# First attention layer: partial sums kept in PSUM per block of nodes instead of added into SBUF after every slot

## The chip, the cores and the metric

The kernel runs on one NeuronCore of a Trainium2 chip. TensorE (PE) multiplies matrices into PSUM, eight banks of 512 fp32 per partition; VectorE (DVE) and ScalarE (ACT) work elementwise on SBUF and PSUM; GpSimd (POOL) here issues indirect gathers; SyncE (SP) issues the other DMAs. The engines run their own programs and wait for one another on semaphores. The metric is the device time of one execution in microseconds; less is better.

## The reference, cut to what matters

Two graph layers are computed over 3125 nodes and 100000 edges sorted by destination. The change touches the first attention of the second layer (8 heads of 64):

```python
feat = (x @ W).reshape(n_nodes, H, D)
e = leaky_relu(el[src] + er[dst], 0.2)
m = segment_max(e, dst)
ex = exp(e - m[dst])
denom = segment_sum(ex, dst)
out = segment_sum((ex / denom[dst])[:, :, None] * feat[src], dst)
```

The kernel divides last: for each node it sums `ex * [feat, 1]` over the node's edges, 8 heads of 65 columns (520 in all), and the 65th column of a head is the denominator.

## The kernel before, in words

Nodes lie in `NB` = 25 blocks of 128, edges in chunks of 256. A **slot** is one chunk as far as it lies in one block; there are `NS` = 415 slots, about 17 to a block, in rising order of block. The slot stage handles each as follows.

- POOL (`gather_heads`, line 1824) issues two indirect gathers, each of 128 rows of 2080 bytes of `t2`, into one of `NR` = 10 buffers `hpair` (parts of `a3` and `wts`); it waits until TensorE has done slot s - 10 (`head_mm`).
- SP (line 2030) loads the 128x16 exponentials of the slot into `exb`, four slots in a group, up to eight slots ahead (`head_ex`).
- ACT (lines 1365 and 1367) makes the two one-hot matrices of the slot, 128x128 each, with two instructions for each: Abs(iota - destination) into `oht`, then Relu(1 - that) into `oh`, a ring of four slots.
- DVE (line 1170) multiplies the gathered 128x1040 by the exponentials, which it first copies to PSUM, four slots at a time (line 1167).
- TensorE (line 1715) runs four fp32 matrix products of 260 columns, which the profile lists as eight matmuls; with `start` and `stop` a slot's sum stands alone in one of three PSUM regions `pbig`.
- DVE (line 1158, `add_heads`) adds that 128x520 to the row of its block in `acc1` (part of `a0`) at a register address. In its program the add of slot s - 2 stands behind the multiply of slot s.

While the first 163 slots run, TensorE also does 89 **looks** (lines 1630 and 1632, 16 bf16 matmuls of 200 columns each), which pick the source term of edges for the second half of the exponentials; DVE reduces each (line 856) and spreads sweeps, maxima and leaky ReLU of that half (lines 830 to 951) between the slots. Looks and slots take the three regions of `pbig` in turn (`RING`): each use waits until the use three places before has been read. ACT takes the exponential of the second half (`exps(1)`) some slots after DVE has finished; the order of all this is fixed in the program, by `AFTER` (which look follows which slot) and `MARK` (at which slot a step of DVE ended). The edges of the second half are first needed at slot 195. Before the stage `acc1` is cleared by one memset of DVE (line 997) and two of POOL.

Of the kernel before, what the change touches and what calls it, by code (L numbers as in the profile page):

```python
# [13 lines left out]
P = 128  # L14
# [22 lines left out]
W1 = 520  # L37
OT = {8: 3, 1: 4}
# [132 lines left out]
def program(nc, x, src, dst, ew, w1, b1, g1, be1, w2, b2, g2, be2, wp, bp,  # L171
            gw1, al1, ar1, gw2, al2, ar2, out):
    ctx = ExitStack()
    with ctx:
# [33 lines left out]
        br = sb("br", [4, P], I32)  # L208
# [25 lines left out]
        oht = sb("oht", [P, 2, P])  # L234
# [30 lines left out]
        pbig = [ps[:, 1024 * i:1024 * (i + 1)] for i in range(3)]  # L265
        tp = [bank(4), bank(5)]
# [76 lines left out]

        foundb = [t.rearrange("p b w -> p (b w)")[:, 0:128] for t in (stat[:, :, :], den[:, :, :])]
# [67 lines left out]
        head_oh, head_mm, head_add, head_mul, head_ex = (sem(n) for n in ("head_oh", "head_mm", "head_add", "head_mul", "head_ex"))  # L412
        act_elu, act_heads2 = sem("act_elu"), sem("act_heads2")
        pool_clear, pool_own = sem("pool_clear"), sem("pool_own")
        act_own = sem("act_own")
        V = Steps(sem("vector_step"))
        NCONST = 17
# [14 lines left out]
        def block_of(e, regs, s, table):  # L432

            if s % 4 == 0:
                k = s // P
                e.load(regs, table[k:k + 1, s % P:s % P + 4])
            return e.snap(regs[s % 4], min_val=0, max_val=NB - 1)

        def vector(e):
            regs = [e.alloc_register(f"vb{i}") for i in range(4)]  # L440
# [148 lines left out]
            def job(name):  # L589
# [93 lines left out]
                elif kind == "plan":  # L683
                    e.wait_ge(pe_prep, PREP["counts"])
                    e.tensor_copy(smalli[:, 0:NB], mp[1][:, 0:NB]).then_inc(*V.inc("counted"))
                    plan(8, 4, NC, 336, 67, "plan2")
                elif kind == "turned":
# [30 lines left out]
                elif kind == "ndl":  # L718
                    e.wait_ge(pe_prep, PREP[name])
                    e.tensor_scalar(ndl[:, name[1], :], mp[1][:, :], -1.0, None, ALU.mult).then_inc(*V.inc(name))  # L720
                elif kind == "slots2":
                    e.wait_ge(pe_prep, PREP["slots2"])
                    e.tensor_copy(br[:, :], mp[1][0:4, 0:P]).then_inc(*V.inc())
                    e.tensor_copy(cr[:, :], mp[1][0:4, P:2 * P]).then_inc(*V.inc("slots2"))

# [123 lines left out]
            def found(H, i, to):  # L849
# [4 lines left out]
                pp = pbig[i % 3 if H == 1 else RING["look", i][0]][:, 0:per * stride].rearrange("p (t w) -> p t w", w=stride)  # L854
# [100 lines left out]
            def first_half():  # L955
# [40 lines left out]
                e.wait_ge(*V.last())  # L996
                e.memset(acc1[:, 0:3136], 0.0).then_inc(*V.inc("acc clear"))
# [150 lines left out]
            e.wait_ge(pool_clear, 2)  # L1148

            def add_heads(s):  # L1150
                e.wait_ge(head_mm, s + 1)
                if s:
                    e.wait_ge(head_add, s)
                else:
                    e.wait_ge(*V("acc clear"))
                b = block_of(e, regs, s, br)
                d = acc1[:, bass.ds(b * W1, W1)].rearrange("p (u w) -> p u w", u=2)
# [20 lines left out]
            add_heads(NS - 2)  # L1178
            add_heads(NS - 1)
            e.wait_ge(head_add, NS)  # L1180
# [45 lines left out]
        uses = [("look", i_) for i_ in range(LOOKS_A)] + [("look", i_) for i_ in AFTER[-1]]  # L1226
        for s_ in range(NS):
            uses += [("slot", s_)] + [("look", i_) for i_ in AFTER.get(s_, ())]
        RING = {use: (n_ % 3, uses[n_ - 3] if n_ >= 3 else None) for n_, use in enumerate(uses)}
# [4 lines left out]
        def scalar(e):  # L1234
# [119 lines left out]

            exps(0)
            for s in range(NS):
                so = s % 4
                for k in range(2):
                    if s >= 4:
                        e.wait_ge(head_mm, s - 3)  # L1360
                    elif s == 0 and k == 0:
                        e.wait_ge(*V("slots2"))
# [738 lines left out]
```

## Time and profile before

| | us |
|---|---|
| median of three runs | 3218.97 (3212.55 to 3219.84) |
| the profiled execution | 3221.76 |
| its span, first to last instruction | 3218.8 |
| in the span: slots 1 to 164, with looks | 1494 to 1994 |
| slots 165 to 177 | 1994 to 2048 |
| slots 178 to 414, no looks | 2048 to 2733 |
| DVE busy / TensorE busy over the span | 2334.0 / 2639.7 |

The span is followed by stretches in time, since the stages have different limits: the graph convolutions up to about 1250, the scores of the attention to 1490, the slot stage to 2733, the second attention behind it. A slot counts as done when its last matmul ends.

### The profile page before, as it was taken

The numbers are of one execution on the slowest core, as the hardware profiler recorded it, in microseconds if no ns is written. First come the engines' busy times: TensorE is split into PE (matmuls) and PEld (weight loads), VectorE is DVE, ScalarE is ACT, GpSimd is POOL, SyncE is SP. The second block draws the span as 40 slices with busy tenths as digits, with TensorE's granted clock in tenths as the row PEclk, the third lists the DMA queues.
The fourth block names the chain that finished last, engine by engine and source line by source line (L and its number), as shares of the span: only waits on it lengthen the run. The fifth ranks groups of instructions, "written<-read, shape, count | busy, mean of one in ns | idle before, by whom it ended". The sixth has DMA issues, their size and how long they took to land.

```text
span 3218.8 us, 51543 instructions
## 1 busy us (share of the span) xinstructions
PE 2639.7 (82%) x18059; PEld 1978.5 (61%) x18059; DVE 2334.0 (73%) x3121; ACT 1279.2 (40%) x3089; POOL 999.5 (31%) x1235
## 2 busy tenths in 40 slices
PE   4777777999899998886888987777676777866999
PEld 2666665545455555785777776555555555765888
DVE  7999997797334444987777878866666666785786
ACT  6888885020001112003444444444444444403343
POOL 3000000111102223006666666666666664003000
PEclk8999999999999999997999999998889889967999
DMA  4444446434478783215666776666676666052453
GB/s 136 185 171 179 170 180 236 137 115 132 138 241 260 254 261 108 86 50 176 190 186 192 194 196 176 181 188 183 182 188 181 188 183 170 24 182 61 155 164 108
DMA packets 311101, 538.20 MB, mean 167 GB/s; under 512 B 108482, under 2 KB 213460, under 8 KB 310596
## 3 DMA queue, kind: packets, MB, share of 16 engines
q1 hardware_dynamic: 241700, 309.63, 29.3%
q0 software_dynamic: 69152, 225.28, 24.9%
q8 instruction: 152, 2.49, 0.3%
q14 instruction: 97, 0.79, 0.1%
HBM read 420.89 MB, written 115.11 MB: 167 GB/s over the span
## 4 chain that ended last, share of the span: by engine, by line
PE 56%; DVE 27%; issue 5%; ACT 5%; another core or an unknown queue 4%; DMA 2%; POOL 1%; DVEq 0%; SPq 0%; ACTq 0%; POOLq 0%
PE ps L1715 22%; PE ps L1496 14%; PE ps L1703 9%; DVE a L586 8%; PE ps L1632 5%; DVE a L581 3%; DVE a L582 3%; PE ps L1400 2%; DVE a L1158 2%; DVE a L830 1%; ACT oht L1365 1%; PE ps L1630 1%; ACT oh L1367 1%; PE ps L1522 1%
## 5 line engine op out<-in xcount | busy, mean ns | idle before, releaser
L1715 PE MATMUL ps<-a,oh 128*128 128x260 f32 x2008 | 510.8, 408 | 148.8 <-ACT oh L1367 56.9
L1824 POOL DMA_INDIRECT a<-t,mid x502 | 482.5, 961 | 443.6 <-DVE cin L940 167.8
L1365 ACT ACTIVATE oht<-iota,mid 128x128 f32<-128x128 f32 x830 | 333.3, 402 | 639.3 <-PE ps L1715 425.4
L1496 PE MATMUL ps<-a 128*128 128x512 f32 x1200 | 554.4, 602 | 13.2 <-DVE a L763 13.2
L1715 PEld LDWEIGHTS ps<-a,oh 128*128 128x128 f32 x2008 | 390.3, 202 | 251.0 <-ACT oh L1367 110.2
L1158 DVE TENSOR_TENSOR a<-a,ps 128x520 f32 x415 | 286.6, 691 | 286.8 <-PE ps L1715 196.0
L1715 PE MATMUL ps<-wts,oh 128*128 128x260 f32 x1312 | 345.7, 419 | 97.5 <-DVE wts L1170 40.1
L1463 PE MATMUL ps<-a 128*128 128x200 bf16 x1568 | 319.9, 255 | 108.7 <-issue 53.3
L1824 POOL DMA_INDIRECT wts<-t,mid x328 | 312.5, 953 | 187.5 <-issue 79.4
L1715 PEld LDWEIGHTS ps<-wts,oh 128*128 128x128 f32 x1312 | 265.3, 209 | 165.3 <-ACT oh L1367 59.8
L1496 PEld LDWEIGHTS ps<-a 128*128 128x128 f32 x1200 | 218.6, 192 | 220.8 <-issue 214.6
L1774 POOL TENSOR_SCALAR rstd<-mv 128x1 f32<-128x1 f32 x75 | 30.2, 403 | 915.3 <-DVE mv L473 913.0
L1170 DVE TENSOR_TENSOR a<-a,ps 128x1040 f32<-128x1040 f32 x251 | 308.6, 1230 | 2.2
L1465 PE MATMUL ps<-a 128*128 128x100 bf16 x1568 | 297.9, 208 | 0.0
L1466 PE MATMUL ps<-a 128*128 128x100 bf16 x1568 | 297.7, 208 | 0.0
L1703 PE MATMUL ps<-a,wts 128*128 128x257 f32 (+1 forms) x1250 | 277.0, 384 | 21.2 <-DVE wts L1109 21.2
L1703 PEld LDWEIGHTS ps<-a,wts 128*128 128x128 f32 (+1 forms) x1250 | 235.8, 189 | 60.5 <-DVE wts L1109 23.2
L1367 ACT ACTIVATE oh<-oht 128x128 f32<-128x128 f32 x830 | 257.0, 310 | 26.2
L586 DVE TENSOR_TENSOR a<-a,mid 128x4800 bf16<-128x4800 bf16 x98 | 260.5, 2658 | 3.4
L1463 PEld LDWEIGHTS ps<-a 128*128 128x128 bf16 x1568 | 152.6, 97 | 162.8 <-issue 152.5
L1285 ACT ACTIVATE a<-ps 128x400 f32<-128x400 f32 x392 | 194.4, 496 | 69.6 <-PE ps L1466 67.7
L1287 ACT ACTIVATE ps<-mzero 128x400 f32<-128x400 f32 x392 | 198.8, 507 | 12.5
(327 smaller groups left out, 3920.6 us busy)
## 6 DMA issues: line engine op xcount, KB each, us to landing
a<-at_d SPq DMA_DIRECT2D x60, 1280.0 KB, 6.1
at_d<-a SPq DMA_DIRECT2D x49, 800.0 KB, 3.3
mt_d<-a SPq DMA_DIRECT2D x49, 800.0 KB, 4.9
a<-mt_d SPq DMA_DIRECT2D x30, 1280.0 KB, 6.1
a<-trlo_d SPq DMA_DIRECT2D x49, 512.0 KB
ot_d<-a SPq DMA_DIRECT2D x49, 320.0 KB, 6.0
a<-ot_d SPq DMA_DIRECT2D x49, 256.0 KB, 3.3
a<-t,mid POOLq DMA_INDIRECT x502
```

The costliest lines, as they stand in the source:

```text
L586: e.tensor_tensor(mvr[:, r, :, 0:3], bc(mvr[:, r, :, 3:4], five), bc(w, five), ALU.mult).then_inc(*V.inc(("weighted", b)))
L1158: e.tensor_tensor(d, d, pbig[RING["slot", s][0]].rearrange("p (u w) -> p u w", u=2)[:, :, 0:260], ALU.add).then_inc(head_add, 1)
L1170: e.tensor_tensor(bv, bv, col(exps_ps[:, s % 8, :], 65), ALU.mult).then_inc(head_mul, 1)
L1365: e.activation(oht[:, k, :], iota[:, :], ACT.Abs, bias=ndl[:, k, s:s + 1]).then_inc(*own.inc())
L1367: e.activation(oh[:, so, k, :], oht[:, k, :], ACT.Relu, bias=1.0, scale=-1.0).then_inc(head_oh, 1)
L1463: e.matmul(ps[:, bass.ds(c, W2)].rearrange("p (k d) -> p k d", k=2), lo, mvr[:, b % RB, g, 2:4, :, z], start=False, stop=True, skip_group_ ...
L1465: e.matmul(ps[:, bass.ds(c, WC)], lo, mvr[:, b % RB, g, 0, :, z], start=False, stop=True, skip_group_check=True)
L1466: e.matmul(ps[:, bass.ds(c, WC)], lo, mvr[:, b % RB, g, 1, :, z], start=False, stop=True, skip_group_check=True).then_inc(slot_done, 1)
L1496: m = e.matmul(acc[f].rearrange("p (x d) -> p x d", x=8), X[:, hi, P * f:P * (f + 1)], a, start=(hi == 0), stop=end, skip_group_check=True)
L1703: m = e.matmul(bank(u + j)[0:p, 0:D + 1], coef[t % R2][:, P * j:P * j + p], feat2[:, hi, :], start=(hi == 0), stop=(hi == NB - 1))
L1715: t = e.matmul(pbig[b][:, 512 * u:512 * u + 260], oh[:, so, k, :], hrows[2 * r + k][:, 260 * u:260 * (u + 1)], start=(k == 0), stop=(k == 1))
L1824: e.indirect_dma_start(out=hrows[2 * r + k], out_offset=None, in_=t2, in_offset=bass.IndirectOffsetOnAxis(ap=srci[:, k, s:s + 1], axis=0)) ...
```

## The change

It does five things.

1. All slots of a block add into one PSUM region: the matmuls lose `start`, and their address is a register (`acc_at`, 0 or 1024 columns), so that successive blocks alternate between `pbig[0]` and `pbig[1]`. DVE's add and its three-region ring are gone.
2. ACT no longer makes one-hots. It fills a region (`prepare`, line 1365 of the new file) and copies it out into `acc1` when the run of slots has ended (line 1381): a **run** is what one block has in one of two walks over all 25 blocks. The first walk ends at slot `S0` = 178 whatever block that falls in, so that `exps(1)` has a fixed place behind run 24; the second starts at block 0 again, putting back into PSUM what `acc1` holds. There are 50 runs; those without slots are copied out and prepared like the others.
3. DVE makes the one-hots: two tensor_scalar is_equal of 128x128, in a ring of ten (`RO`).
4. TensorE waits for the run's region (`acc_ready`, against a register) and loads two tables of registers every four slots.
5. Looks use `pbig[2]` alone; the memsets of `acc1` are gone; DVE reads a look three slots behind it rather than two.

The diff, cut to its core:

```diff
+RO = 10
+S0 = 178
+RUNS = 2 * NB
...
+        def run_sum(r):
+            return pbig[(r + 1) % 2].rearrange("p (u w) -> p u w", u=2)[:, :, 0:W1 // 2]
...
 (vector)
-                e.wait_ge(*V.last())
-                e.memset(acc1[:, 0:3136], 0.0).then_inc(*V.inc("acc clear"))
...
-            def add_heads(s):
-                e.wait_ge(head_mm, s + 1)
...
-                e.tensor_tensor(d, d, pbig[RING["slot", s][0]].rearrange("p (u w) -> p u w", u=2)[:, :, 0:260], ALU.add).then_inc(head_add, 1)
             for s in range(NS):
-                r = s % NR
+                r, so = s % NR, s % RO
+                if s >= RO:
+                    e.wait_ge(head_mm, s - RO + 1)
+                for k in range(2):
+                    e.tensor_scalar(ohs[so][:, k, :], iota[:, :], ndl[:, k, s:s + 1], None, ALU.is_equal).then_inc(head_oh, 1)
...
-                if s >= 2:
-                    add_heads(s - 2)
-                    for i in AFTER.get(s - 2, ()):
-                        found_b(i)
+                for i in AFTER.get(s - LOOK_LAG, ()) if s >= LOOK_LAG else ():
+                    found_b(i)
...
-            add_heads(NS - 2)
-            add_heads(NS - 1)
-            e.wait_ge(head_add, NS)
+            e.wait_ge(acc_out, RUNS)
...
+        LOOK_LAG = 3
+            u_ = i_ % 3 if i_ < LOOKS_A + len(AFTER[-1]) else 2
...
 (scalar)
+            def prepare(r):
+                phase, b = divmod(r, NB)
+                i = acc1[:, W1 * b:W1 * (b + 1)].rearrange("p (u w) -> p u w", u=2) if phase else bc(mzero[:, :].rearrange("p (a b) -> p a b", a=1), [P, 2, W1 // 2])
+                e.activation(run_sum(r), i, ACT.Copy).then_inc(acc_ready, 1)
...
-                    e.activation(oht[:, k, :], iota[:, :], ACT.Abs, bias=ndl[:, k, s:s + 1]).then_inc(*own.inc())
-                    e.wait_ge(*own.last())
-                    e.activation(oh[:, so, k, :], oht[:, k, :], ACT.Relu, bias=1.0, scale=-1.0).then_inc(head_oh, 1)
-                if s == MARK["less max", 1] + 4:
+            for r in range(RUNS):
+                if r % 4 == 0:
+                    e.load(run_regs, run_end[0:1, r:r + 4])
+                e.reg_alu(run_at, run_regs[r % 4], 1, ALU.max)
+                e.wait_ge(head_mm, run_at)
+                b = r % NB
+                e.activation(acc1[:, W1 * b:W1 * (b + 1)].rearrange("p (u w) -> p u w", u=2), run_sum(r), ACT.Copy).then_inc(acc_out, 1)
+                if r + 2 < RUNS:
+                    e.wait_ge(acc_out, r + 1)
+                    prepare(r + 2)
+                if r == NB - 1:
                     exps(1)
...
 (tensor)
+                e.reg_alu(lim, lim_regs[s % 4], 1, ALU.max)
+                e.wait_ge(acc_ready, lim)
                 e.wait_ge(head_oh, 2 * s + 2)
                 e.wait_ge(head_mul, s + 1)
-                e.wait_ge(*(V("found", 8, before[1]) if before[0] == "look" else (head_add, before[1] + 1)))
...
-                        t = e.matmul(pbig[b][:, 512 * u:512 * u + 260], oh[:, so, k, :], hrows[2 * r + k][:, 260 * u:260 * (u + 1)],
-                                     start=(k == 0), stop=(k == 1))
+                        t = e.matmul(ps[:, 512 * u:512 * u + 2048][:, bass.ds(c, 260)], ohs[so][:, k, :], hrows[2 * r + k][:, 260 * u:260 * (u + 1)],
+                                     start=False, stop=True, skip_group_check=True)
...
 (gpsimd)
-            e.memset(acc1[:, 3136:6400], 0.0).then_inc(pool_clear, 1)
-            e.wait_ge(*V("leaky", 0))
-            e.memset(acc1[:, 6400:], 0.0).then_inc(pool_clear, 1)
...
 (sync)
-            written = min(MARK["less max", 1] + 12, 192)
+            written = S0 + 8
```

DVE in the last part of the slot stage, before: `br` is the table of block numbers, `gh_in7` says that a gather has landed.

```order
L1170 TENSOR_TENSOR wts<-wts,ps 128x1040 [waits gh_in7]
L437 ISA [waits head_add,head_mm]
L1158 TENSOR_TENSOR a0<-a0,ps 128x520
L1167 COPY ps<-exb 128x64 [waits ex_in6,ex_in5,ex_in7,ex_in4,gh_in8]
L1170 TENSOR_TENSOR wts<-wts,ps 128x1040 [waits head_ex]
L437 ISA [waits head_add,head_mm]
L1158 TENSOR_TENSOR a0<-a0,ps 128x520
L1170 TENSOR_TENSOR wts<-wts,ps 128x1040 [waits gh_in9]
```

The same place after (line 1170 of the new file is the one-hot, line 1179 the multiply):

```order
L1170 TENSOR_SCALAR a4<-iota,mid 128x128 [waits head_mm]
L1170 TENSOR_SCALAR a4<-iota,mid 128x128
L1179 TENSOR_TENSOR wts<-wts,ps 128x1040 [waits gh_in7]
L1170 TENSOR_SCALAR a4<-iota,mid 128x128 [waits head_mm]
L1170 TENSOR_SCALAR a4<-iota,mid 128x128
L1176 COPY ps<-exb 128x64 [waits ex_in2,ex_in1,ex_in3,ex_in0,gh_in8]
L1179 TENSOR_TENSOR wts<-wts,ps 128x1040 [waits head_ex]
```

Behind each multiply stood an add that waits for TensorE's slot s - 2; now two one-hots stand ahead of it, which wait for slot s - 10.

TensorE in the part with looks, before:

```order
L1715 MATMUL ps<-a3,oh 128x260 [waits vector_step,head_mul,head_oh]
L1715 MATMUL ps<-a3,oh 128x260 x3
L1715 MATMUL ps<-a3,oh 128x260 [waits head_add,head_mul,head_oh]
L1715 MATMUL ps<-a3,oh 128x260 x3
L1630 MATMUL ps<-small,dst_n 128x200 [waits vector_step]
L1632 MATMUL ps<-tbl,dst_n 128x200 x3
```

and after (ISA is an address worked out from a register):

```order
L1649 MATMUL ps<-tbl,src_n 128x200 x3
L1737 REGISTER_ALU
L1744 ISA [waits head_mul,head_oh,acc_ready]
L1744 MATMUL ps<-wts,a4 128x260 x2
L1744 ISA
L1744 MATMUL ps<-wts,a4 128x260 x2
L1647 MATMUL ps<-small,src_n 128x200 [waits vector_step]
L1649 MATMUL ps<-tbl,src_n 128x200 x3
...
L1735 TENSOR_LOAD acc_at
L1736 TENSOR_LOAD acc_lim
```

The slot's wait for a read of its region is replaced by one for the run's region; every look now waits for DVE's reading of the look before it (`vector_step`).

ACT where the two walks meet, after (before, this engine had only the pairs of lines 1365 and 1367 there):

```order
L1381 ACTIVATE a0<-ps 128x520 [waits head_mm]
L1365 ACTIVATE ps<-a0 128x2x260 [waits acc_out]
L1377 TENSOR_LOAD run_end
L1378 REGISTER_ALU
L1381 ACTIVATE a0<-ps 128x520 [waits head_mm]
L1365 ACTIVATE ps<-a0 128x2x260 [waits acc_out]
L1360 ACTIVATE a1<-a1 128x1564 [waits vector_step] x2
L1378 REGISTER_ALU
L1381 ACTIVATE a0<-ps 128x520 [waits head_mm]
L1365 ACTIVATE ps<-a0 128x2x260 [waits acc_out]
```

The two exponentials of the second half stand between the copies of run 24 and run 25.

## Rows read from the trace of the kernel before

**Rows 1.** Busy time by stretch: start:end, length, then each engine's busy us.

```profile
core 0: us, PE busy (x) PEld busy (x) DVE busy (x) ACT busy (x) POOL busy (x), PEclk, DMA share, GB/s
1494.00:1994.00 500.00, 444.10 (x2730) 372.82 (x2729) 395.73 (x497) 233.16 (x656) 311.23 (x327) 0.97 0.69 190
1994.00:2048.00 54.00, 33.13 (x114) 24.22 (x113) 53.58 (x70) 20.95 (x55) 29.04 (x28) 0.84 0.54 141
2048.00:2733.00 685.00, 494.13 (x1895) 383.56 (x1893) 437.38 (x532) 333.19 (x937) 430.94 (x456) 0.91 0.68 185
```

**Rows 2.** Waits, stretch 2048 to 2733: who waited for whom, us, times, longest.

```profile
ACT oht L1365 <- PE ps L1715: 195.1, 69, 4.6
```

**Rows 3.** Groups of instructions, stretch 2048 to 2733: count, busy us, mean ns, idle before.

```profile
L1824 POOL DMA_INDIRECT a<-t,mid x274 | 258.9, 945 | 146.6 <-issue 71.9 <-PE ps L1715 43.1 <-remote 31.6
...
L1158 DVE TENSOR_TENSOR a<-a,ps 128x520 f32 x237 | 163.9, 691 | 244.6 <-PE ps L1715 160.3 <-remote 74.4 <-issue 9.6
...
L1170 DVE TENSOR_TENSOR wts<-wts,ps 128x1040 f32<-128x1040 f32 x93 | 114.5, 1231 | 0.8
L1167 DVE COPY ps<-exb 128x64 f32<-128x64 f32 x58 | 12.7, 220 | 0.0
```

**Rows 4.** Timeline, 2261 to 2274: start us, length us, engine, line, [idle before].

```profile
2261.90 7.33 PE L1715 MATMUL ps<-a,oh 128*128 128x260 f32 x32
2265.83 1.23 DVE L1170 TENSOR_TENSOR a<-a,ps 128x1040 f32<-128x1040 f32 x1
2268.57 0.95 POOL L1824 DMA_INDIRECT a<-t,mid  x1 [0.30 <-issue]
2270.69 0.40 ACT L1365 ACTIVATE oht<-iota,mid 128x128 f32<-128x128 f32 x1 [4.52 <-PE ps L1715]
2270.81 0.70 DVE L1158 TENSOR_TENSOR a<-a,ps 128x520 f32 x1 [3.75 <-PE ps L1715]
2270.93 0.96 POOL L1824 DMA_INDIRECT a<-t,mid  x1 [1.41 <-PE ps L1715]
```

**Rows 5.** Groups of instructions, stretch 1494 to 1994.

```profile
L856 DVE TENSOR_REDUCE stat<-ps 128x32 f32<-128x800 f32 x44 | 43.4, 987 | 38.1 <-remote 30.1 <-PE ps L1632 6.0 <-issue 1.7
```

**Rows 6.** Busy time by stretch while TensorE does only looks.

```profile
1360.00:1440.00 80.00, 77.32 (x880) 76.19 (x880) 67.65 (x84) 0.00 (x0) 0.00 (x0) 1.00 0.20 55
```

**Rows 7.** Groups in the stretch 80 to 480, matmuls at register addresses, ScalarE's clears and copies.

```profile
L1463 PE MATMUL ps<-a 128*128 128x200 bf16 x1361 | 276.3, 254 | 96.3 <-issue 47.5 <-ACT ps L1287 20.5 <-DVE a L586 20.0
...
L1287 ACT ACTIVATE ps<-mzero 128x400 f32<-128x400 f32 x342 | 173.4, 507 | 10.9
L1285 ACT ACTIVATE a<-ps 128x400 f32<-128x400 f32 x342 | 169.6, 496 | 58.0 <-PE ps L1466 56.3
```

**Rows 8.** Groups in the stretch 2745 to 2790, the same shapes on DVE and ACT.

```profile
L1196 DVE TENSOR_TENSOR a<-a,den 128x512 f32<-128x512 f32 x18 | 12.3, 684 | 0.0
...
L1293 ACT ACTIVATE yt<-ps 128x512 f32<-128x512 f32 x18 | 10.7, 597 | 0.1
...
L1200 DVE TENSOR_SCALAR a<-a 128x512 f32<-128x512 f32 x17 | 7.3, 427 | 1.8
```

**Rows 9.** Timeline, 1462 to 1490, of DVE, POOL, ACT and SP.

```profile
1464.13 3.48 DVE L951 TENSOR_TENSOR a<-a 128x1564 f32<-128x1564 f32 x2
1464.40 2.34 POOL L1824 DMA_INDIRECT a<-t,mid  x1 [0.31 <-issue]
1467.65 1.51 ACT L1353 ACTIVATE a<-a 128x1564 f32<-128x1564 f32 x1 [0.19 <-DVE a L951]
1476.24 0.95 POOL L1824 DMA_INDIRECT wts<-t,mid  x1 [0.30 <-issue]
1476.76 0.29 DVE L1012 TENSOR_TENSOR a<-a,stat 128x128 f32<-128x128 f32 x1
1482.92 2.79 DVE L856 TENSOR_REDUCE den<-ps 128x32 f32<-128x800 f32 x3 [5.87 <-remote]
1484.17 6.96 SPq L2030 DMA_DIRECT2D exb<-ex_d  x10
```

More of the change, by code:

```diff
@@ L342, in program @@
         hrows = [t[:, W1 * k:W1 * (k + 1)] for t in hpair for k in range(2)]
+        run_no = small[0:4, 128:256]
+        ohs = [oh[:, i, :, :] for i in range(4)] + [a4[:, 544 + 256 * i:800 + 256 * i].rearrange("p (k n) -> p k n", k=2) for i in range(RO - 4)]
         foundb = [t.rearrange("p b w -> p (b w)")[:, 0:128] for t in (stat[:, :, :], den[:, :, :])]
@@ L686, in job @@
                     plan(8, 4, NC, 336, 67, "plan2")
+                    e.tensor_scalar(run_endf[:, 0:NB - 1], small[0:1, 65:64 + NB], float(S0), None, ALU.min).then_inc(*V.inc())
+                    e.tensor_copy(run_endf[:, NB:2 * NB - 1], small[0:1, 65:64 + NB]).then_inc(*V.inc())
+                    e.memset(run_endf[:, NB - 1:NB], float(S0)).then_inc(*V.inc())
+                    e.memset(run_endf[:, 2 * NB - 1:64], float(NS)).then_inc(*V.inc())
+                    e.wait_ge(*V.last())
+                    e.tensor_copy(run_end[:, :], run_endf[:, :]).then_inc(*V.inc("run ends"))
                 elif kind == "turned":
@@ L1225, in program @@
             AFTER.setdefault(-1 if i_ < LOOKS_A + 9 else int((i_ - LOOKS_A - 9) * 1.85), []).append(i_)
[L1226 to L1229, printed above, removed]
+        LOOK_LAG = 3
+        RING = {}
+        for i_ in range(len(LOOKUPS[8])):
+            u_ = i_ % 3 if i_ < LOOKS_A + len(AFTER[-1]) else 2
+            before_ = [k_ for k_ in range(i_) if RING[k_][0] == u_]
+            RING[i_] = (u_, before_[-1] if before_ else None)
         MARK, SLOT = {}, [-1]
@@ L1353, in exps @@
                     e.activation(fvs[:, xx:y], fvs[:, xx:y], ACT.Exp).then_inc(act_exp, 1)
+            def prepare(r):
+                phase, b = divmod(r, NB)
+                i = acc1[:, W1 * b:W1 * (b + 1)].rearrange("p (u w) -> p u w", u=2) if phase else bc(mzero[:, :].rearrange("p (a b) -> p a b", a=1), [P, 2, W1 // 2])
+                e.activation(run_sum(r), i, ACT.Copy).then_inc(acc_ready, 1)
             exps(0)
[L1356 to L1362, printed above, removed]
[L1363 to L1368 removed]
+            e.wait_ge(*V("run ends"))
+            for i in AFTER[-1][-3:]:
+                e.wait_ge(*V("found", 8, i))
+            prepare(0)
+            prepare(1)
+            run_regs = [e.alloc_register(f"run_end{i}") for i in range(4)]
+            run_at = e.alloc_register("run_at")
+            for r in range(RUNS):
[9 more added lines that the diff above has]
+                if r == NB - 1:
                     exps(1)
@@ L1617, in look @@
                 nbf = small[:, 0:2 * W].bitcast(BF16).rearrange("p (t w) -> p t w", t=4)
-                b, before = (i % 3, ("look", i - 3) if i >= 3 else None) if H == 1 else RING["look", i]
+                b, before = (i % 3, i - 3 if i >= 3 else None) if H == 1 else RING[i]
                 pp = pbig[b][:, 0:per * stride].rearrange("p (t w) -> p t w", w=stride)
@@ L1625, in look @@
                 if before is not None:
-                    e.wait_ge(*(V("found", H, before[1]) if before[0] == "look" else (head_add, before[1] + 1)))
+                    e.wait_ge(*V("found", H, before))
                 for k in range(m):
@@ L1723, in tensor @@
                     carry_in(1)
-            e.wait_ge(head_add, NS)
+            e.wait_ge(acc_out, RUNS)
             for name, b in HEADS2:
```

62 lines of the change are left out of this document (35 added, 27 removed).

## The prediction

> **What bounds the kernel now.** Read first the busy time by stretch [rows 1]. Slots 1 to 164, with looks beside them, take 500 us, 3.05 a slot; slots 165 to 177 take 54 us with DVE busy for 53.58 of them; the last 237 slots take 685 us, 2.89 each, and there no engine is busy for more than three quarters (PE 494 us, POOL 431, DVE 437, ACT 333). So the last stretch is bound by a loop of waits. The waits [rows 2] and the idle time ahead of groups [rows 3] show which: ACT's first one-hot step stands 195 us for TensorE, and DVE's add 244.6 us, which is 1.03 us a slot. The timeline [rows 4] shows one turn of it. TensorE runs four slots from 2261.90 to 2269.23, slots 252 to 255, 7.33 / 4 = 1.83 us each. DVE ends its multiply at 2267.06 and then stands in the add of slot 253, whose matmuls by that spacing ended near 2265.7; it starts at 2270.81, and ACT, DVE and POOL all start within 0.24 us of one another. TensorE's signal came about 5 us late, 1.2 us after POOL had ended its last gather (2269.52) and stood still. I take from this that TensorE's signals are held back while POOL issues gathers without a pause, and come when it stops. Everything that waits closely on them (DVE's add two slots behind, ACT's ring of four) stops with them.
>
> A milder reading is that only the end of the matmuls is shown too early. The Trainium skill bears on it, Perfetto Trace Analysis, "Tensor Engine Instruction (MATMUL, LD_WEIGHTS)": TensorE's end in a profile is worked out from the instruction's size, not observed. By that rule a slot could really cost TensorE the 2.89 us and the last stretch would not get shorter at all; the row on the looks' stretch speaks against it, where the same matmuls and 0.77 us of looks fit into 3.05 us.
>
> Behind the loop stands POOL: a gather takes 945 ns [rows 3] and 0.30 of issue [rows 4], so 2 x 1.25 = 2.50 us a slot. That is the floor of the last stretch if nothing waits. In the first stretch TensorE comes near too: 1.83 for the slot, and 16 matmuls of a look at 77.32 / 880 = 0.088 us [rows 6], 1.41 us, for 89 looks in 163 slots 0.77 us: 2.60 together.
>
> **What changes, part by part.** I go against the profiled execution, 3221.76 us; the median is 2.8 less, which I take off at the end.
>
> *DVE.* Its add goes, 0.69 us [rows 3], and with it the wait on slot s - 2. Two one-hots come. No row has them: 128x512 of the same operation takes 0.427 us against 0.684 for a two-input one [rows 8], so 0.11 each by its columns alone is the lower end and 0.29, what a two-input 128x128 takes [rows 9], the upper one. I take 0.24 as nearer to the latter, where the fixed part shows, 0.48 for two. DVE has then 1.23 + 0.48 + 0.22 / 4 = 1.77 us a slot, under POOL's 2.50: hidden, except in slots 165 to 177, where it is full, (0.69 - 0.48) x 13 = 3 us gained. It now waits for slot s - 10, as POOL does.
>
> *ACT.* Its four one-hot steps go. No slot waits on it any more but at the walks' seam.
>
> *The last stretch, cadence.* What still waits for late signals is POOL (ten slots deep), DVE's one-hots (ten, two slots behind POOL), and ACT at the end of a run, with a run of 17 slots as cover. POOL issues up to ten slots; a gather lands, is multiplied and used some 3 slots behind. If signals come only when POOL stops, each stop frees about 7 to 8 slots instead of the 4 to 5 now, for a stop of 1.4 us [rows 4] to 2.2. That makes 2.50 + 0.2 = 2.70 us a slot. The lower end is 2.50, the upper 2.89 as now.
>
> *The seam, added.* When slot 177 is done, its block is number 10. ACT must copy out and prepare runs 10 to 33 before region 35, where slot 178 adds: 24 pairs. A pair is two copies of 520 columns: 0.60 for 512 columns [rows 8], 0.61 each, plus 0.09 between (400 columns take 0.50 and 0.51 [rows 7]), 1.31 us; and two exponentials of 1.51 [rows 9]. That is 24 x 1.31 + 3.0 = 34.5 us in which TensorE stands. POOL stands too, its ring being full, until slot 178 is seen, some 4 us more with TensorE restarting on its lower clock. Nothing covers this. Ten slots lie ready then; POOL has 227 to issue, and the last takes 7 us to land, be multiplied, added and copied out. The last stretch is 34.5 + 4 + 7 = 46 (rounded) plus 227 x 2.70 = 613, so 659 us against 685: 26 gained. The cadence at which it would gain nothing is (685 - 46) / 227 = 2.81.
>
> *The first stretch.* The floor is TensorE's 2.60 plus addresses from registers. In the stretch of register-addressed matmuls the idle time ahead of 1361 of them is 47.5 us of issue, at most 96.3 in all [rows 7]: 0.035 to 0.07 each, up to 0.1 a slot for two. Against it, looks have one region instead of a share of three: look i + 1 waits for DVE's reduce of look i, 0.99 us, and that for a signal of TensorE; DVE already stands 38.1 us ahead of 44 of these, 30.1 of them for signals with no clear sender [rows 5], late ones. Two slots, 3.7 us, usually lie between looks, so a signal over 2.5 us late stops TensorE. I take 2.80, between 2.65 and the present 3.05, nearer the lower since the add and ACT's ring no longer stop it: 164 x 0.25 = 41 us gained.
>
> *At nothing.* The memsets that go: DVE waits 5.87 us behind its own [rows 9] and the exponentials' loads only start at 1484.17, so the stage starts when it did. Five small instructions more for the tables stand in DVE's program beside convolution work bound by TensorE. TensorE's two table loads every four slots stand ahead of a wait while 1.83 us of matmuls run; uncovered they would cost what the range of the first stretch has in it. The late load of the small piece is needed only in the second attention.
>
> Sum: 41 + 3 + 26 = 70 us; 3221.76 - 70 = 3152, for the median **3149 us**.
>
> **The rivals.**
> *Freed entirely.* POOL never waits, the first stretch falls to 2.65: 66 + 3 + (685 - 46 - 568 = 71) = 140 us, 3079. For it: ten slots are 25 us and the longest wait of ACT is 4.6 [rows 2]. Against: nothing shows that a hold ends before POOL stops.
> *The gathers set the pace (slower).* Both stretches run near 3 us a slot though TensorE's load differs by 0.77 us; DMA share is 0.69 and 0.68 in both [rows 1]. If the pace belongs to gathers and signals as a whole and stays, the first stretch gains nothing and the last is 46 + 227 x 2.89 = 702, 17 slower, less the 3 of the middle: 3233. The seam decides: above 2.81 the last stretch loses. Against: at 2.50 us a slot POOL has nothing to do for a seventh of the last stretch, so something else holds the pace.
> *The one-hots hold POOL up.* A gather took 2.34 us beside a long two-input operation of SBUF, 0.95 beside one of 0.29 us [rows 9]. Were POOL stopped for all of 0.48 us a slot, it would need 2.98: 11 gained in the first stretch, 3 in the middle, 46 + 676 - 685 = 37 lost in the last: 3242. By the Trainium skill, SBUF — State Buffer, "Who interferes with whom", this is the rule: a VectorE operation in a two-port mode and a GpSimd one lock a shared pair of ports for the whole instruction. The short row disagrees with it, the long one agrees.
> *Looks stop more often.* The single region makes late signals stop every look; the first stretch goes to 3.2, 25 lost, against 29 gained elsewhere: 3215.
> *It does not do what it says.* If slot 178 waited for runs that are ready, the seam would vanish; the order shows the pairs as they were counted, so I give this nothing.
>
> **How the numbers follow.** Forecast 0.50 (its own range 3105 to 3190), freed entirely 0.17, gathers set the pace 0.16, one-hots hold POOL 0.07, looks stop 0.10. The range, 3075 to 3242, leaves out the outer halves of the outer cases and what their unknown costs add. About 0.3%, 10 us, can be told from no change. Faster 0.66, the forecast and the freed case; same 0.11, mostly the looks case; slower 0.23, the two others.
>
> **What would show it.** In the changed kernel's profile: slots 178 to 414 from seam to end at 2.5 to 2.8 us each; a gap of TensorE of 35 to 40 us at slot 178 with ACT full in it; DVE's idle time ahead of multiplies (gathers), no more on TensorE, in the last stretch; one-hots of 0.2 to 0.29 us and gathers still 945 ns; the first stretch at 2.65 to 2.9 with DVE's reduce as its largest wait. The forecast is wrong if POOL still idles 0.4 us a slot, if gathers last over 1.1 us, or if the seam is over 60 us.

## The result, and the profile after

The changed kernel takes 3236.43 us (median, 3228.79 to 3243.24) against 3216.99 us (3210.42 to 3223.03) of the kernel before: a ratio of 1.0062, interval 1.0047 to 1.0078, so slower by about 20 us. The forecast was 3149 us, a gain. The time lies inside the stated range, near its upper end, and the sign is wrong.

Busy time by stretch of the changed kernel's profiled execution (its own time 3237.48 us): start:end, length, then each engine's busy us and instructions, granted TensorE clock, DMA share, GB/s. The stretches are slots 1 to 164, 165 to 177, the seam at slot 178, and the rest.

```profile
core 0: us, PE busy (x) PEld busy (x) DVE busy (x) ACT busy (x) POOL busy (x), PEclk, DMA share, GB/s
1494.00:2004.00 510.00, 445.18 (x2722) 382.80 (x2721) 363.15 (x662) 10.90 (x18) 312.09 (x327) 0.94 0.68 186
2004.00:2052.00 48.00, 31.23 (x109) 22.55 (x107) 44.95 (x73) 1.21 (x2) 34.30 (x28) 0.85 0.60 163
2052.00:2087.00 35.00, 3.93 (x9) 2.86 (x9) 16.84 (x33) 31.17 (x52) 2.03 (x2) 0.50 0.20 65
2087.00:2756.00 669.00, 523.04 (x1889) 409.99 (x1887) 386.75 (x738) 16.36 (x27) 431.50 (x454) 0.85 0.69 185
```

Beside [rows 1]: the first stretch became 10 us longer, not 41 shorter; the second is 5 to 6 shorter; slots 178 to 414 took 685 us and take 35 + 669 = 704. From slot 178 on, the seam included, DVE has 34 us less to do and ACT 286 less, and neither is worth anything. The data rate is 185 GB/s, as before.

Groups of instructions from slot 178 to 414: count, busy us and mean ns, then idle time before them and what ended it.

```profile
L1854 POOL DMA_INDIRECT a<-t,mid x274 | 260.4, 950 | 137.4 <-issue 73.0 <-remote 60.7 <-PE ps L1744 3.7
L1744 PE MATMUL ps<-a,oh 128*128 128x260 f32 x768 | 222.0, 441 | 61.6 <-issue 56.5 <-DVE a L1170 3.8
L1179 DVE TENSOR_TENSOR a<-a,ps 128x1040 f32<-128x1040 f32 x137 | 169.6, 1238 | 125.9 <-DMA a<-t,mid 114.4 <-issue 10.3
L1170 DVE TENSOR_SCALAR a<-iota,mid 128x128 f32<-128x128 f32 x270 | 66.6, 295 | 4.1 <-PE ps L1744 4.1
L1381 ACT ACTIVATE a<-ps 128x520 f32<-128x520 f32 x14 | 8.5, 604 | 648.7 <-remote 442.1 <-PE ps L1744 206.7
```

The waits of [rows 2, 3] have moved as meant: DVE no longer stands for TensorE but for gathers, ACT for ends of runs. But GpSimd's gathers, 950 ns and 0.30 of issue as before, still have stops ahead of them ("remote": a signal for which the profile finds no sender close before it). And TensorE, which hardly waits for anybody now, has 56.5 us of idle time with no cause shown in one group alone.

The timeline round one stop of GpSimd shows both. Start us, length us, engine, line, operation, [idle before, and what ended it]:

```profile
2371.79 5.20 PE L1744 MATMUL ps<-a,oh 128*128 128x260 f32 x23
...
2377.20 0.95 POOL L1854 DMA_INDIRECT wts<-t,mid  x1 [0.30 <-issue]
...
2377.51 0.38 PE L1744 MATMUL ps<-a,oh 128*128 128x260 f32 x1 [0.51 <-issue]
...
2378.45 0.95 POOL L1854 DMA_INDIRECT wts<-t,mid  x1 [0.30 <-issue]
2378.94 0.38 PE L1744 MATMUL ps<-a,oh 128*128 128x260 f32 x1 [1.05 <-issue]
...
2380.35 0.47 PE L1744 MATMUL ps<-a,oh 128*128 128x260 f32 x1 [1.04 <-issue]
...
2381.78 1.36 PE L1744 MATMUL ps<-a,oh 128*128 128x260 f32 x3 [0.96 <-issue]
2382.06 0.95 POOL L1854 DMA_INDIRECT wts<-t,mid  x1 [2.66 <-remote]
2382.93 3.45 PE L1744 MATMUL ps<-a 128*128 128x260 f32 x9
```

The gather at 2382.06 is the first of slot 289 and needs slot 279 done, whose last matmul by this record ended at 2371.30: GpSimd stood from 2379.40, and started 10.8 us after the work that it waited for. Meanwhile TensorE stops between the matmul passes of slot 283, where it waits for no semaphore, four times for 0.5 to 1.05 us. In this trace's records of that semaphore three updates stand together, at 2381.80, 2381.89 and 2381.99, just ahead of the gather: the signals themselves came late and in a bunch. (Some 20 of its 415 records are missing, so they can't be paired one by one.)

Counted over both profiles of each kernel, slots 200 to 414: before, GpSimd stopped 66 and 67 times, started 5.4 and 5.1 us (mean) after the matmuls it needed had ended, and was idle in these stops for 116 and 113 us; after, 47 and 46 times, 10.5 and 10.6 us late, 101 and 102 us. Of each stop 0.30 us is the ordinary time of issue; without it the stops come to 96 and 93 us before and 87 and 88 after. The longer rings of DVE and ACT made fewer and longer stops, and the slot stays at 2.88 us (before 2.90).

The seam, same view: ACT's first pairs and the end of it.

```profile
2052.41 0.60 ACT L1381 ACTIVATE a<-ps 128x520 f32<-128x520 f32 x1 [33.84 <-PE ps L1744]
...
2053.04 0.61 ACT L1365 ACTIVATE ps<-mzero 128x520 f32<-128x520 f32 x1
2053.59 0.59 ACT L1381 ACTIVATE a<-ps 128x520 f32<-128x520 f32 x1
...
2054.74 0.59 ACT L1381 ACTIVATE a<-ps 128x520 f32<-128x520 f32 x1
...
2069.82 2.89 ACT L1360 ACTIVATE a<-a 128x1564 f32<-128x1564 f32 x2
...
2083.44 6.28 PE L1744 MATMUL ps<-wts,a 128*128 128x260 f32 x16 [31.07 <-ACT ps L1365]
...
2087.54 0.95 POOL L1854 DMA_INDIRECT wts<-t,mid  x1 [32.56 <-PE ps L1744]
```

24 pairs of 1.15 and the two exponentials: TensorE begins again at 2083.44, 31.1 us after slot 177 ended (2052.4), and GpSimd at 2087.54, 35.1 us after it.

In the first stretch the waits that grew are those round the looks (who waited for whom: us, times, longest):

```profile
DVE den L874 <- remote: 68.3, 24, 5.5
POOL a L1854 <- PE ps L1744: 63.9, 34, 11.6
...
PE ps L1647 <- DVE den L874: 35.6, 12, 5.5
...
DVE stat L874 <- remote: 32.0, 10, 5.8
...
PE ps L1647 <- DVE stat L874: 18.7, 5, 5.3
```

The same waits in the kernel before, 1494 to 1994:

```profile
DVE stat L856 <- remote: 30.1, 12, 3.8
DVE den L856 <- remote: 18.4, 8, 3.8
PE ps L1630 <- DVE stat L856: 10.0, 8, 2.2
PE ps L1630 <- DVE den L856: 4.9, 5, 2.2
```

DVE's reduces of looks stand 68.3 + 32.0 us for late signals, where they stood 30.1 + 18.4, and TensorE's looks 54 us for these reduces instead of 15. Behind slot 12 alone, a reduce waits 4.74 us and the next look 5.46 for it, and slot 13 ends 11 us after slot 12, where the slots before it took 1.7 to 4.2:

```profile
1530.07 0.99 DVE L874 TENSOR_REDUCE den<-ps 128x32 f32<-128x800 f32 x1 [4.74 <-remote]
1530.40 0.95 POOL L1854 DMA_INDIRECT a<-t,mid  x1 [1.83 <-remote]
...
1531.12 0.35 PE L1647 MATMUL ps<-small,src_n 100*128 100x200 bf16 x1 [5.46 <-DVE den L874]
```

### The profile page after: what moved, and what is told of

Its sections match the earlier page's. It is cut to its first block, busy times and chain, and to the rows that moved or that the text cites. A ratio compares the mean times of both kernels' runs of the same rounds, so it can differ in the third digit from the quotient of the medians.

```text
span 3235.5 us, 50165 instructions
## 1 busy us (share of the span) xinstructions
PE 2677.7 (83%) x18059; PEld 2018.5 (62%) x18059; DVE 2259.8 (70%) x3543; ACT 748.7 (23%) x1529; POOL 1001.8 (31%) x1234
## 4 chain that ended last, share of the span: by engine, by line
PE 46%; DVE 30%; POOL 8%; issue 6%; another core or an unknown queue 5%; ACT 3%; DMA 2%; DVEq 0%; SPq 0%; ACTq 0%; POOLq 0%
PE ps L1513 14%; PE ps L1744 11%; PE ps L1720 8%; DVE a L592 8%; PE ps L1649 5%; POOL a L1854 4%; DVE a L587 3%; POOL wts L1854 3%; DVE a L588 3%; PE ps L1417 2%; DVE a L1179 2%; DVE a L848 2%; DVE wts L1179 2%; PE ps L1647 1%
## 5 line engine op out<-in xcount | busy, mean ns | idle before, releaser
L1744 PE MATMUL ps<-wts,a 128*128 128x260 f32 x1312 | 356.6, 423 | 100.5 <-issue 58.9
L1744 PE MATMUL ps<-a,oh 128*128 128x260 f32 x1344 | 365.5, 424 | 65.0 <-issue 56.5
L1744 PEld LDWEIGHTS ps<-wts,a 128*128 128x128 f32 x1312 | 274.4, 213 | 165.9 <-issue 120.4
L1744 PEld LDWEIGHTS ps<-a,oh 128*128 128x128 f32 x1344 | 280.8, 212 | 131.0 <-issue 84.3
L1381 ACT ACTIVATE a<-ps 128x520 f32<-128x520 f32 x50 | 29.8, 596 | 1207.0 <-PE ps L1744 662.6
L1179 DVE TENSOR_TENSOR wts<-wts,ps 128x1040 f32<-128x1040 f32 x164 | 202.5, 1235 | 86.6 <-DMA wts<-t,mid 73.6
L1744 PE MATMUL ps<-a 128*128 128x260 f32 x664 | 175.8, 414 | 34.2 <-issue 27.0
```

The costliest lines, as they stand in the source:

```text
L1179: e.tensor_tensor(bv, bv, col(exps_ps[:, s % 8, :], 65), ALU.mult).then_inc(head_mul, 1)
L1744: t = e.matmul(ps[:, 512 * u:512 * u + 2048][:, bass.ds(c, 260)], ohs[so][:, k, :], hrows[2 * r + k][:, 260 * u:260 * (u + 1)], start=Fals ...
```

## The experiments

Two theories. **Held signals** (the forecast's): TensorE's signals are held while GpSimd issues without a pause, so whoever stands further back from them loses less. **The gathers' pace** (the rival): something about the gathers allows one slot in 2.88 us, and late signals are how it reaches GpSimd; what one wait loses, another gets. It turned out that the runs met two levels of time for the same program, which became the sharpest comparison of all: the kernel before took 3217, 3215.8 and 3218.9 us on some chips (**late chips**: the first traces', and those that the record numbers 7 and 5), and 3006.6, 3008.2 and 3009.8 on others (**prompt chips**: 9, met twice, and 12). Whether that belongs to the chip itself or to something else that differed there, no run shows. Every ratio below is to the kernel before on the same chip. The changed kernel as it stands was never timed on a prompt chip; the nearest is no_ex below, 3023.93 against 3006.59, so an estimate is 0.6% slower there too.

**The kernels themselves, again.** First the changed one, then the one before, both on a late chip; then the one before on a prompt chip.

> The changed kernel unaltered, timed and profiled again. On the chip of the four runs before, TensorE's signals were not held back: all slots beside gathers took 2.50 to 2.52 us, at GpSimd's floor, and the kernel before took 3006.6 us. If this chip is of that kind: 3024 to 3028 us against 3006 (a ratio of 1.006), slots of 2.51 in both stretches and 34.8 us at slot 178. If it is of the kind of the first traces: 3236 against 3217, slots of 2.88.

> The kernel before unaltered, for its profile on the same chip. Where signals are not held: 3006 us, and the question is where 2.50 is reached. If held signals were the only thing that kept the kernel before from GpSimd's floor, its last 237 slots take 2.50 us each (593 us) with nothing for the change to gain there, and its first 164 about 2.60, so that the change gains 15 us in the first stretch, 3 in the middle and loses 35 at the seam. Where they are held: 3217, slots of 2.89 and 3.05.

Measured: 3234.06 us against 3215.76, ratio 1.0046 (1.0029 to 1.0064); the profiled execution of the kernel before took 3213.39. The last stretch repeats (706 against 684 us from slot 178 to 414). The first lost more, 513 against 495 us where it had been 511 against 500 (from the end of slot 0 to that of slot 164), and the middle gained more, 45 against 57 us.

> The kernel before, for its profile on a chip without holding, 3007 us. If held signals were all that kept it from GpSimd's floor, its last 237 slots take 2.50 us each and the first 164 about 2.55; then the change had nothing to gain there but what ScalarE's and VectorE's rings cost, under 0.1 us a slot, against 35 at the seam. If VectorE's add two slots behind stops it even without holding, its slots are above 2.6. On a chip with holding: 3215 and 2.87 to 2.9.

Measured: 3009.01 us. Stretches of this execution, slots 1 to 164, 165 to 177, 178 to 414:

```profile
1492.00:1909.00 417.00, 414.66 (x2729) 365.97 (x2727) 398.74 (x499) 233.05 (x656) 310.55 (x326) 1.00 0.81 228
1909.00:1963.00 54.00, 33.69 (x111) 24.37 (x110) 53.55 (x68) 21.53 (x55) 32.61 (x29) 0.84 0.55 146
1963.00:2542.00 579.00, 465.23 (x1895) 340.60 (x1895) 445.62 (x531) 332.72 (x936) 432.39 (x456) 1.00 0.79 219
```

The same program, with the same durations (a gather 948 ns, TensorE's slot 1.75 us at full clock), gives 2.51 us a slot from slot 200 on: GpSimd's 2 x 1.25, with no stop at all, and the recorded signals of TensorE's slots stand 14 ns behind the end of the last matmul. Slots 1 to 164 take 2.54 with 89 looks among them. So where signals are prompt the kernel before is already at the floor in both stretches, DVE's add and ACT's ring of four cost it nothing, and the change has little but the middle to gain. TensorE's granted clock in the last stretch is 1.00 here; on late chips, where TensorE has its idle times, it is 0.91 and 0.90 before and 0.85 after.

**The seam.** One walk over the blocks; the second exponentials stand at the place where this graph lets them (run 9 ends with slot 168, run 10 with slot 185), so this version is fitted to this data.

```diff
-RUNS = 2 * NB
+RUNS = NB
...
-                if r == NB - 1:
+                if r == 9:
                     exps(1)
```

(The two tables are made without `S0`.)

> The changed kernel with one walk over the 25 blocks: 25 runs, no run ends at slot 178, and ScalarE's second exponentials stand behind run 9, whose block ends with slot 168 in this graph (so it is fitted to this data). Both theories on the pace agree here, it tests the seam: 24 empty pairs x 1.31 us and two exponentials, 34.9 us in the changed kernel's profile, go, and the pace of the slots stays. Expected 3236 - 32 = 3204 us (3198 to 3210), so 13 us under the kernel before; no gap of TensorE over 5 us at slot 178. If what follows the seam had gained from it (ten slots lie ready, 227 instead of 237 are left to fetch), up to 28 us of the gap come back and the time is about 3225 to 3230.

Measured: 2994.34 against 3006.59, ratio 0.9958 (0.9945 to 0.9972), on a prompt chip. Three more runs of it, the last on a late one:

> The changed kernel with one walk (25 runs, second exponentials behind run 9), as in the first call, for a chip on which signals are held. The seam of 34.8 us goes and the pace stays 2.88 us for the 236 slots from 178 on (a pace set by held signals asks for no seam): 3234 - 32 = 3202, 14 under the kernel before. But ten slots lay ready behind the seam and went at 1.78 us each; without the seam these 11 us come back: 3213, about the kernel before. On a chip without holding: 2994 against 3006.

> The changed kernel with one walk (25 runs, second exponentials behind run 9), once more for a chip on which signals are held. If the seam simply adds to the pace: 3234 - 32 = 3202, a ratio of 0.996. If what lay ready behind the seam (ten slots at 1.78 us) was a gain that came from it: 3213, 0.999 to 1.001. On a chip without holding: 0.995 as in the two calls before.

Measured, prompt again: 2993.75 (0.9946, 0.9930 to 0.9963) and 2995.93 (0.9957, 0.9943 to 0.9971).

> The changed kernel with one walk, once more for a chip on which signals are held. If the seam simply adds to the pace: 3234 - 32 = 3202, a ratio of 0.996. If what lay ready behind the seam (ten slots at 1.78 us) was a gain that came from it: 3213, 0.999 to 1.001. On a chip without holding: 0.995, as three times before.

Measured on a late chip: 3203.53 against 3218.91, ratio 0.9949 (0.9931 to 0.9967). Its last stretch (POOL busy, clock, share and GB/s are the last five numbers):

```profile
2046.00:2723.00 677.00, 525.33 (x1898) 412.85 (x1896) 403.45 (x771) 19.39 (x30) 436.63 (x458) 0.84 0.69 187
```

677 us against 704 and 706, and 3203.53 us in all against 3236.43 and 3234.06 of the changed kernel on other late chips: the whole is 31 to 33 us shorter, as the seam alone would have it (3202 to 3204), and not 3213. In the last stretch itself 27 to 29 us of the seam's 31 to 35 show. GpSimd stops 44 times, 10.5 us late, 2.89 us a slot. Without the seam the rest of the change is worth 15 us on a late chip and 12 to 14 on a prompt one. This beats both kernels.

**Whose pace it is.** All of these take something out from slot 200 on, and fit the waits to it. First on a prompt chip: no gathers, and, in a run of its own, no loads of exponentials.

```diff
-            for s in range(NR, NS):
+            for s in range(NR, 200):
                 gather_heads(s)
```

> The changed kernel without the gathers of slots 200 to 414, which use the rows that lie in their buffers: everything else of a slot is done. Slots 200 to 414 took 2.88 us each. If signals are held back by gathers, or gathers set the pace, the slots fall to TensorE's or VectorE's own time, 1.83 to 2.0 us: 215 x 0.95 = about 200 us less, 3035. If TensorE's matmuls really last longer than the profile shows and gathers don't matter, they stay at 2.6 to 2.9 us: 3180 to 3240.

Measured: 2858.70 us, one execution; from slot 200 to 414 it took 375 us, 1.75 each. That is TensorE's own time for a slot, with DVE beside it. The expectation had been written for a late chip.

> The changed kernel without SyncE's loads of exponentials from slot 200 on (old ones are used). If these loads of 64-byte pieces and SyncE's register work are what slows signals or gathers, the slots fall to 2.50 to 2.60 us: 60 to 80 us less, 3155 to 3175. If it is gathers alone, 2.85 to 2.9 us stay: 3225 to 3240.

Measured: 3023.93 us; 2.51 a slot. The loads set nothing there; on a late chip this wasn't tried.

Then half of the matmuls, on a prompt and on a late chip:

```diff
-                for u in range(2):
+                for u in range(2 if s < 200 else 1):
                     for k in range(2):
                         t = e.matmul(...)
```

> The changed kernel without the second half (columns 260 to 519) of the matmuls of slots 200 to 414. If signals are held until GpSimd stops, the number of matmuls has no part in it: 2.8 to 2.9 us a slot, 3220 to 3237. If TensorE's own true pace beside gathers is 2.88 us and the end in the profile is shown too early, the slots fall to GpSimd's 2.50 us: 215 x 0.38 = 81 us less, 3155.

> The changed kernel without the second half of the matmuls of slots 200 to 414, again, for a chip of the other kind. Where signals are not held: 2.50 us a slot as before (3026 us). Where they are: 2.8 to 2.9 (3220 to 3237) by the theory of held signals; 2.50 (3155) if TensorE's true pace beside gathers is 2.88.

Measured: 3025.98 (prompt) and 3226.81 (late, 7 us under the whole one), one execution each. Between the multiplies of slots 210 and 414 a slot took 2.51 and 2.86 us. On the late chip:

```profile
2145.00:2740.00 595.00, 391.58 (x832) 222.89 (x832) 353.64 (x674) 15.13 (x25) 389.44 (x411) 0.62 0.69 189
```

TensorE's granted clock is 0.62 (0.85 with whole slots), so its busy time fell less than its columns; still it is idle for a third of the stretch, and the pace did not move: TensorE's number of matmuls has no part in it, and the "milder reading" of the forecast, that a slot really costs TensorE 2.89 us of matmuls, falls. The next run says the same, with all eight matmuls.

Half of the gathers, on the late chip:

```diff
-                for k in range(2):
+                for k in range(2 if s < 200 else 1):
                     e.indirect_dma_start(...)
```

> The changed kernel with one gather of 128 rows instead of two in slots 200 to 414. GpSimd's floor falls to 1.25 us. Where signals are not held TensorE sets the pace at 1.75 (slots 200 to 414 took 375 us without any gather): 161 us less than the changed kernel. Where signals are held until GpSimd stops, each slot brings half of the holding: 1.8 to 2.0 us a slot, 190 to 230 us less. If bytes moved per time are the limit (532 KB in 2.88 us), 1.75 as well; if TensorE's own true pace is 2.88, nothing is gained.

Measured: 2982.10 us, one execution, 252 less than the changed kernel. That is the case of a limit on the gathers (1.75 us a slot); held signals had 190 to 230 less. Slots 200 to 414:

```profile
2125.00:2500.00 375.00, 375.00 (x1713) 325.07 (x1711) 342.80 (x683) 15.15 (x25) 197.62 (x208) 1.00 0.60 155
```

TensorE is full, 1.75 us a slot, to the microsecond the same as without gathers. The timeline, GpSimd's rows:

```profile
2202.57 0.95 POOL L1855 DMA_INDIRECT a<-t,mid  x1 [0.80 <-PE ps L1745]
...
2204.32 0.95 POOL L1855 DMA_INDIRECT a<-t,mid  x1 [0.81 <-PE ps L1745]
...
2206.07 0.95 POOL L1855 DMA_INDIRECT wts<-t,mid  x1 [0.81 <-PE ps L1745]
```

GpSimd now waits ahead of every gather, for TensorE, and starts 0.27 us after the end of the slot it needs; from slot 225 on it was over 0.5 us late only 8 times in 190. On the same chip, in the same execution, the first stretch was as slow as ever (507 us), but here the lateness is nearly gone, and so are TensorE's stops inside a slot. A gather every 1.75 us is fine; one every 1.25 is what a late chip does not keep up, and it settles at one every 1.44.

**A break or the bytes.** Register operations were meant as a break in GpSimd's issuing:

> One walk, and four register operations of GpSimd behind each slot's two gathers, a break of some 0.1 to 0.3 us in its issuing. If signals pass whenever GpSimd does not issue for a moment, GpSimd never stands for them and the slots take 2.50 plus the break, 2.6 to 2.8: 20 to 90 us less than one_walk2. If only a stop on a wait, or a pause of more than about 0.5 us, lets them pass, the break adds to 2.88 or lies in the stops: 0 to 60 us more. On a chip without holding it costs its length, 415 x 0.1 to 0.3.

> One walk, and sixteen register operations behind each slot's gathers, a break of 0.4 to 1.2 us. By held signals: no stops of GpSimd are left, TensorE's signals come within 1 us of its last matmul's end, and the slots take 2.50 plus the break. If signals stay late by 5 to 10 us even so, it is not GpSimd's issuing that holds them but the traffic of the transfers.

Measured on a prompt chip: 2993.30 (0.9953, 0.9936 to 0.9970) and 2995.31, the time between gathers 0.305 us as without them. They made no break, so these two runs say nothing of the theories. A small operation of GpSimd's own made one:

```diff
+                if s >= 8:
+                    e.wait_ge(pool_pause, s - 7)
+                e.tensor_scalar(pause[:, s % 8:s % 8 + 1], mhalf[:, :], 1.0, None, ALU.mult).then_inc(pool_pause, 1)
```

> One walk, and one small GpSimd operation (128x1, 0.26 to 0.4 us) behind each slot's two gathers, in its own queue of instructions, so that its issuing breaks for that long. Where signals are held: if any break of issuing lets them pass, GpSimd no longer stands for them and a slot takes 2.50 + 0.3 to 0.5 = 2.8 to 3.0, with TensorE's signals no more than one slot late and no stop of GpSimd; if the break is too short or bytes are the cause, stops stay (46 of them, 2 us each) and the slots rise to 3.1 to 3.4. Where they are not held: 2.8 to 3.0, about 150 us more.

Measured on a prompt chip: 3067.13, ratio 1.0202 (1.0185 to 1.0219): 2.69 us a slot in the last stretch, less than the 2.8 to 3.0 expected.

> One walk, and one small GpSimd operation (128x1) behind each slot's two gathers, which made a slot 2.69 us on a chip without holding, 0.19 over the floor. Where signals are held: if a break of issuing of this length lets them pass, GpSimd no longer stands and the slots take 2.69 to 2.75, 0.13 to 0.19 less than now, 30 to 60 us less than one_walk4; if the break is too short or the bytes under way are the cause, its stops stay and the slots take 2.9 to 3.1, 0 to 70 us more. Where they are not held: 3067, as before.

Measured on the late chip of one_walk4: 3211.70, ratio 0.9977 (0.9962 to 0.9991), 8 us over one_walk4; their profiled executions are 3.7 us apart, 2.8 of them in slots 165 to 177. Slots 178 to 414:

```profile
2047.00:2725.00 678.00, 539.86 (x1896) 405.49 (x1896) 402.32 (x771) 18.54 (x29) 502.44 (x686) 0.83 0.70 186
```

This decides between the theories, for the last stretch. On a prompt chip the break adds 0.19 us to each slot; here it adds nothing to the last stretch (678 against 677), and the stops shrink in its place: 31 instead of 44. Without the ordinary idle time ahead of a gather (0.30 us, in this kernel 0.16) they come to 50 us instead of 88, a difference of 38 where 215 x 0.19 = 41 were put in. Signals are not prompter (13.1 us late when GpSimd stops). By held signals either the break should have been added to each slot, 3.08 us, or the stops should have gone, 2.69 to 2.75; it was 2.88. So the time a slot takes is given, and a stop is only what is left of it.

Half of the bytes with the same number of rows (from slot 200 on):

```diff
-                    e.indirect_dma_start(out=hrows[2 * r + k], out_offset=None, in_=t2, ...
+                    e.indirect_dma_start(out=hrows[2 * r + k][:, 0:260], out_offset=None, in_=t2.rearrange("n (h w) -> (n h) w", h=2), ...
```

> One walk, and gathers of rows of 1040 bytes instead of 2080 in slots 200 to 414: the same number of rows and of instructions, half the bytes. If signals are held by GpSimd's issuing: the same pace as one_walk2, 2.85 to 2.9 us. If the bytes under way hold them, or the transfers set the pace: 2.50, 80 us less. On a chip without holding 2.50 in both.

> One walk, and gathers of rows of 1040 bytes instead of 2080 in slots 200 to 414, same number of rows and instructions. Where signals are held: 2.85 to 2.9 us a slot if GpSimd's issuing holds them; 2.50 if the bytes under way do, 80 us less. Where they are not: 2.50 in both, 2993 us.

Measured: 2993.27 and 2997.30, one execution each, both on prompt chips, 2.50 us a slot at 110 GB/s instead of 217. There the pace is GpSimd's issue and not the bytes; whether bytes or rows are what a late chip counts stays open.

## Why the prediction was wrong, point by point

- **What bounds the kernel.** That TensorE's signals come late beside back-to-back gathers was right for the chip at hand, and that GpSimd's 2.50 us is the floor was shown by the prompt chips. That the stops for these signals were the cause of the 2.89 was wrong.
- **The last stretch, cadence: the step that failed.** It took the stop as the cause: deeper rings, so 7 to 8 slots for each stop of 1.4 to 2.2 us, so 2.70 (by its own terms 2.68 to 2.81). A stop now frees 215 / 47 = 4.6 slots (before 3.3) and costs 87 / 47 = 1.9 us over the issue (before 1.4), while the signals' lateness doubled with the rings. With 35.1 for the seam and 7 at the end, (704 - 42) / 227 = 2.92 us, over the 2.81 from which the change loses. This is the rival "the gathers set the pace", whose 702 us for this stretch is what was measured (704). That its 3233 in all lies so near 3236 is in part luck: it had nothing for the first stretch, which lost 11 us, nor for what lies behind the stage, which gained 7. I had argued against it that GpSimd idles for a seventh of the stretch, so that something else must hold the pace. pause2 shows why that does not follow: idle time in a stage that something else holds to its pace shrinks by what is put into it.
- **The first stretch.** 41 us gained were forecast, 10 are lost (18 in the second pair of profiles). The same step: that the add and ACT's ring stopped it. On prompt chips they cost nothing (417 us for the stretch with them, 416 without, in one_walk3). What is lost looks like the looks' rival in small: late signals stop looks at their single region, 54 us of TensorE's waits for DVE's reduces, where before it waited 15 for them. The rival's price had been 25 us. No run gave the looks their regions back, so this part is argued from the waits and not shown.
- **The middle.** 3 us forecast, 5 gained in the first traces, 13 in the second pair, 7 on prompt chips (one_walk3: 54 to 46 us). The two one-hots are in the rows 0.48 us together, exactly as estimated, but overlap the multiply at both ends: in one_walk4 multiplies follow each other at 1.54 us where DVE is full, 0.31 more than their own 1.23.
- **The seam.** 34.5 us of standing and 4 for GpSimd's start were forecast, 31 and 4 measured, a pair 1.15 us rather than 1.31: the 0.09 us between two copies, for which no row was given, does not occur. one_walk4 shows its price by itself: 704 to 677 us in the last stretch.
- **At nothing.** Nothing was found against it: the stage's first slot ends at 1492.8 (before 1494.6).
- **The one-hots and GpSimd.** The one-hots left the gathers at 950 ns (before 945), so that rival did not occur. Its two rows are of two-input operations, and a one-hot has one input, so they bore on it only loosely. A gather beside two long two-input operations at slot 177 took 4.20 us in one_walk4. By the Trainium skill, SBUF — State Buffer, "Who interferes with whom", a VectorE instruction with two inputs in SBUF contends with a GpSimd instruction that reads SBUF, and not with one that only writes it. A gather's row numbers lie in SBUF, so the trace agrees for the long ones, 4.20 us against 0.95, if that counts as reading. The forecast had quoted the section's sentence on two-port modes, which that section denies to this kind of operation. Whether the one-hots ran in such a mode no run shows.
- **The size of the miss.** 3236 - 3149 = 87: 51 in the first stretch and 45 in the last, less 2 or 3 of the middle, 2 by which the stage began earlier, and some 7 by which the part behind slot 414 became shorter (486 to 479 us; the second pair has 482 to 479).

What stays open is what in a late chip sets one gather per 1.44 us, bytes (185 GB/s) or rows (128), and why it reaches TensorE, whose instructions need nothing of GpSimd. A limit on how its instructions are supplied is not excluded; no run took that apart. Two things speak against it: with half the gathers TensorE took its instructions at 1.75 us a slot without a stop, and the packets of the larger instruction queue lasted as long on late as on prompt chips (1.04 us mean in after, 1.05 in before_again2).

## What to carry to other kernels

Before you make rings deeper to ride out late signals, ask whether something else holds the stage to its pace: put a small delay into the idle engine, and if the time does not change, its idle time is not there to be won. A stop that is the same sum in fewer pieces gains nothing. And a walk over empty cases has its full price wherever TensorE waits for its last step: here leaving it out is worth more than all the rest of the change, and the kernel without it is 0.4 to 0.5% under the kernel before on every chip that it met.

## What was not expected of the hardware

- The same kernel takes 3217 us on some chips and 3007 on others, 7%, nine tenths of it in the two stretches with gathers issued back to back (at the end 2.90 against 2.51 us a slot); the DMA queues moved 185 GB/s in the last stretch on the ones and 217 to 219 on the others. The ratio of one_walk's kernel to the one before was alike on both (0.9949 on a late chip, 0.9946 to 0.9958 on prompt ones).
- On late chips TensorE itself stops inside a slot, between passes that wait for no semaphore: 115 idle times over 0.3 us within 550 us of the changed kernel, 123 us in all, in clusters about 17 us apart. In the kernel before, on a late chip, there was none ahead of a pass that waits for nothing; whether its waits hid them is not shown. With half the gathers there was not one.
- Landing was not what was late: 2.3 to 2.5 us (median) from the end of a slot's second gather instruction to the last landing recorded for it on late chips, 2.8 on prompt ones.
